# Attention scores in bursts of two duos over six PSUM banks, one routing scatter per step, in a fused attention and expert kernel

## The reference

```
x = x + tanh(g_xattn) * attention(layernorm(x), ctx, mask)   # 16 heads of 64
x = x + tanh(g_ffn)   * experts(layernorm(x))                # 8 experts, 2 per row

attention: q = ln(x) Wq, k = ctx Wk, v = ctx Wv
           softmax(q k^T / 8, masked) v Wo
experts:   top 2 of ln(x) Wg^T, softmax over the two,
           sum of weight * W3[e] (silu(W1[e] x) * (W2[e] x))
```

## Time and profile before

| what | value |
|---|---|
| median of three runs | 665.11 us (661.04 to 665.76) |
| the profiled execution | 661.78 us, span 660.0 us |
| busy share PE, DVE, ACT, POOL | 94%, 60%, 44%, 47% |
| chain that ended last, by engine | PE 77%, POOL 6%, DMA 5%, issue 4%, DVE 4% |
| attention steps 0 to 127 (from 33.0 to 402.6 us) | PE busy nearly without a gap |
| 402 to 432 us (end of attention) | PE busy 23.4 of 30.0 us, DMA share 0.99 |
| 480 to 640 us (expert tiles) | PE busy 160.0 of 160.0 us |

### The profile page before, as it was taken

The page is one execution under the profiler, slowest core; times in us unless marked ns, Lnnn a source line. Parts: engine busy times, 40 slices in busy tenths (PEclk is TensorE's granted clock), DMA queues, the critical chain, the costliest instruction groups (busy, mean ns, idle before and its releaser), DMA issues.

```text
span 660.0 us, 10752 instructions
## 1 busy us (share of the span) xinstructions
PE 622.1 (94%) x2958; PEld 346.2 (52%) x2959; DVE 393.6 (60%) x1187; ACT 287.7 (44%) x744; POOL 309.2 (47%) x272
## 2 busy tenths in 40 slices
PE   4599999999999999999999999699999999999994
PEld 2244445454555544455554555256666666666663
DVE  3767788888987878988769977333251212221211
ACT  1556665656555564564545554023322222222221
POOL 2345565555564587564685564502464222222221
PEclk9989999999999999999999998899999999999998
DMA  8904577676766776757677569969556322333221
GB/s 273 333 1 104 144 168 170 142 167 146 163 149 150 161 186 163 166 130 184 134 193 179 135 158 249 269 186 377 161 142 131 49 41 42 47 48 48 46 23 22
DMA packets 92652, 95.37 MB, mean 144 GB/s; under 512 B 11056, under 2 KB 86704, under 8 KB 92592
## 3 DMA queue, kind: packets, MB, share of 16 engines
q1 hardware_dynamic: 69968, 71.64, 41.9%
q10 hardware_dynamic: 15840, 14.07, 9.4%
q0 software_dynamic: 6784, 8.95, 8.2%
HBM read 27.72 MB, written 12.36 MB: 61 GB/s over the span
## 4 chain that ended last, share of the span: by engine, by line
PE 77%; POOL 6%; DMA 5%; issue 4%; DVE 4%; ACT 2%; ACTq 1%; POOLq 0%; SPq 0%; DVEq 0%
PE ps_s L1396 17%; PE ps_s L1216 14%; PE ps_o L1241 13%; PE ps_o L1424 8%; PE ps_a L1149 7%; PE ps_a L1251 7%; POOL probs L525 3%; POOL x_regrouped L513 2%; DMA out_dram<-yg,ids 2%; PE ps_o L1227 2%; PE ps_t L1417 2%; PE ps_s L1143 2%; DVE blocksT L996 2%; DMA probsT<-blocksT 1%; DMA wk_sb<-Wk_dram 1%
## 5 line engine op out<-in xcount | busy, mean ns | idle before, releaser
L525 POOL TENSOR_TENSOR probs<-probs,inv_sum 128x802 f32<-128x802 f32 x128 | 194.8, 1524 | 154.5 <-DVE inv_sum L975 153.7
L636 ACT ACTIVATE probs<-probs,neg_max 128x401 f32<-128x401 f32 x256 | 159.3, 624 | 147.1 <-DVE neg_max L984 147.0
L984 DVE CUSTOM_DVE_ANT_0 probs<-ps_s,biases 128x401 f32<-128x401 f32 x256 | 136.9, 573 | 52.5 <-PE ps_s L1216 51.6
L1396 PE MATMUL ps_s<-w_sb,xgT 128*128 x296 | 139.5, 594 | 1.4 <-ACT xgT L732 1.4
L996 DVE STREAM_TRANSPOSE blocksT<-probs 128x832 f32<-128x832 f32 x128 | 133.2, 1040 | 9.0 <-POOL probs L525 9.0
L564 POOL DMA_INDIRECT out_dram<-yg,ids x36 | 56.0, 1555 | 159.4 <-DVE yg L1108 136.5
L1241 PE MATMUL ps_o<-probsT,v_sb 128*64 128x512 f32 x512 | 125.0, 612 | 4.4 <-DMA probsT<-blocksT 4.4
L1216 PEld LDWEIGHTS ps_s<-kT,qT 64*128 64x128 f32 x1024 | 82.9, 187 | 78.6 <-DVE neg_max L984 42.2
L1216 PE MATMUL ps_s<-kT,qT 64*128 64x201 f32 (+1 forms) x1024 | 122.0, 357 | 1.4 <-issue 1.4
L1096 DVE TENSOR_TENSOR gated<-ps_s,silu 128x512 f32<-128x512 f32 x37 | 25.6, 692 | 117.5 <-PE ps_s L1396 112.1
L1396 PEld LDWEIGHTS ps_s<-w_sb,xgT 128*128 128x128 f32 x296 | 53.0, 191 | 39.5 <-issue 37.9
(11 more groups left out here) (142 smaller groups left out, 420.9 us busy)
## 6 DMA issues: line engine op xcount, KB each, us to landing
probsT<-blocksT SPq DMA_DIRECT2D x285, 96.0 KB
probsT<-blocksT SPq DMA_DIRECT2D x95, 128.0 KB
probsT<-blocksT ACTq DMA_DIRECT2D x99, 96.0 KB
xg<-x_regrouped SPq DMA_DIRECT2D x39, 129.0 KB, 2.1
probsT<-blocksT ACTq DMA_DIRECT2D x33, 128.0 KB
w_sb<-W1T_dram SPq DMA_DIRECT2D x8, 512.0 KB, 9.5
w_sb<-W2T_dram SPq DMA_DIRECT2D x8, 512.0 KB, 10.2
w_sb<-W3T_dram SPq DMA_DIRECT2D x8, 512.0 KB, 10.5
```

Of the source, the lines that this page charges most:

```text
L525: pool.tensor_tensor(duo, duo, inv_sum[:, u:u + 2].unsqueeze(2).to_broadcast([P, 2, LASTK]), ALU.mult)\
L636: act.activation(probs[:, b, 0:LASTK], probs[:, b, 0:LASTK], ACT.Exp, bias=neg_max[:, b:b + 1], scale=-1.0, accum_out=sum_exp[:, b:b + 1]) ...
L984: dve.tensor_tensor_reduce(probs[:, b, 0:LASTK], ps_s[u % 4][:, 0:LASTK], biases[:, tile, :], HD ** -0.5, 3e38, ALU.add, ALU.min, neg_max[ ...
L1396: mm = pe.matmul(bank[:, :], xgT[:, buf, k, :], w_sb[:, bass.ds(expert, 1), (n * KT + k) * FH:(n * KT + k + 1) * FH].squeeze(1), start=(k ...
```

## The change

There are six score banks, `ps_ring`, made of the four `ps_s` and the two `ps_t`. In an even step TensorE issues the scores of duos n and n + 1 one after the other, and in an odd step none. `scores(d)` now waits for the mask of duo d - 3. Everything else keeps its step. Since `ps_t` is taken, the late transposes of normalised x go to `ps_o` and `ps_a` by turns (`xn_bank`), with waits: in steps 8 to 10 for all value copies and for the queries' copy; the queries of step 9 for six of the eight transposes' copies; the queries of step 13 and the first `probs_v` for all eight.

In routing, row groups 0 and 1 (and 3, and the general path) scatter once per stage over stages 22 to 29, row group 2 still twice per stage over 22 to 25. `BESIDE` puts two such stages beside each of the expert tiles 6 to 9, so row group 3 keeps two scatters per tile.

```diff
-LAST_STAGE = 25
-BESIDE = (..., (22,), (23,), (24,), (25,))
+LAST_STAGE = 29
+BESIDE = (..., (22, 23), (24, 25), (26, 27), (28, 29))
...
+        ps_ring = ps_s + ps_t
+        def xn_bank(c):
+            return ps_t[c] if c < 2 else [ps_o, ps_a][c % 2]
...
-                if 22 <= s < 22 + GT:
-                    t = s - 22
-                    for c in range(2):
+                each = 2 if isinstance(r, int) and r == NR - 2 else 1
+                for n in range(each * (s - 22), each * (s - 21)):
+                    if 0 <= n < 2 * GT:
+                        t, c = divmod(n, 2)
                         pool.indirect_dma_start(...)
...
-                    if d >= 2:
-                        pe.wait_ge(masked_ready, 2 * d - 2)
+                    if d >= 3:
+                        pe.wait_ge(masked_ready, 2 * d - 4)
-                            mm = pe.matmul(ps_s[(2 * d + odd) % 4][:, k0:k1], ...
+                            mm = pe.matmul(ps_ring[(2 * d + odd) % 6][:, k0:k1], ...
...
                         if c == 0:
                             pe.wait_ge(v_ready, 2 * NS)
+                            pe.wait_ge(xnT_ready, 2 * NR)
...
-                    if n < DUOS:
+                    if n % 2 == 0 and n < DUOS:
                         scores(n)
+                        scores(n + 1)
                     if n < 2 * NS:
                         values(n)
                     if 2 * NS <= n < 2 * NS + 3:
+                        pe.wait_ge(v_ready, 2 * NS)
+                        pe.wait_ge(q_ready, (n + 2) // 4 + 1)
                         transpose_xn(2 * (n - 2 * NS) + 2)
                         transpose_xn(2 * (n - 2 * NS) + 3)
...
-                        if n // 4 + 1 == HP:
+                        if n == 2 * NS + 1:
+                            pe.wait_ge(xnT_ready, 6)
+                        if n // 4 + 1 == 4:
                             pe.wait_ge(xnT_ready, 2 * NR)
```

More of the change, by code:

```diff
@@ L61 @@
 ROUTE0 = HP * GT + 15
-LAST_STAGE = 25
-BESIDE = ((0, 1, 2, 3), (4, 5, 6, 7), (8, 9, 10), (12, 13, 14), (15, 16), (17, 18, 19, 20, 21), (22,), (23,), (24,), (25,))
+LAST_STAGE = 29
+BESIDE = ((0, 1, 2, 3), (4, 5, 6, 7), (8, 9, 10), (12, 13, 14), (15, 16), (17, 18, 19, 20, 21), (22, 23), (24, 25), (26, 27), (28, 29))
 SCHED_TILES = {7: range(0, 10), 8: range(10, 21)}
@@ L596, in move_xnT @@
                 act.wait_ge(xnT_ps, c + 1)
-                act.copy(xnT[:, c % 2, c // 2 * GQ:(c // 2 + 1) * GQ], ps_t[c % 2][:, :]).then_inc(xnT_ready, 1)
+                act.copy(xnT[:, c % 2, c // 2 * GQ:(c // 2 + 1) * GQ], xn_bank(c)[:, :]).then_inc(xnT_ready, 1)
             def mask_words(c):
@@ L983, in mask_and_max @@
                             dve.wait_ge(blocks_ready, (u - RING_P) // 2 + 1)
-                        dve.tensor_tensor_reduce(probs[:, b, 0:LASTK], ps_s[u % 4][:, 0:LASTK], biases[:, tile, :],
+                        dve.tensor_tensor_reduce(probs[:, b, 0:LASTK], ps_ring[u % 6][:, 0:LASTK], biases[:, tile, :],
                                                  HD ** -0.5, 3e38, ALU.add, ALU.min, neg_max[:, b:b + 1])\
@@ L1159, in transpose_xn @@
                     tile = xn[:, t, :] if c < 2 else xn_late[:, t0 - GT + t, :]
-                    mm = pe.transpose(ps_t[c % 2][:, t * P:(t + 1) * P], tile[:, k * P:(k + 1) * P], ident[:, :])
+                    mm = pe.transpose(xn_bank(c)[:, t * P:(t + 1) * P], tile[:, k * P:(k + 1) * P], ident[:, :])
                 mm.then_inc(xnT_ps, 1)
@@ L1215, in scores @@
                             h0 = odd * HD
-                            mm = pe.matmul(ps_s[(2 * d + odd) % 4][:, k0:k1], qT[h0:h0 + HD, c % 2, t * P:(t + 1) * P],
+                            mm = pe.matmul(ps_ring[(2 * d + odd) % 6][:, k0:k1], qT[h0:h0 + HD, c % 2, t * P:(t + 1) * P],
                                            kT[h0:h0 + HD, c % HP, k0:k1], start=True, stop=True)
```

## The result

The changed kernel takes 658.48 us (median of 8 runs, 656.09 to 660.88) against 665.01 us of the kernel before (8 runs, 661.04 to 666.78): a ratio of 0.9907 with a 95% interval of 0.9881 to 0.9934, 6.2 us less. The profiled execution took 659.66 us, with a span of 657.9.

A forecast was written before the change was run, and what follows sets the result against it. PE, busy 93.00 of 93.00 us in plain attention steps, was taken as the bound, DVE next at 84%. Terms summed to -4.8 us, 661.8 to 657.0, put at 658.6 between run levels; forecast's own range 653 to 663, overall 650 to 668.

The forecast's parts named there:

- Seams: Steady periods: 6 seams for 8 at about 0.2 us each, 11.1 to 10.7 us, -10.8 over 27; list ends -0.4.
- Scatters: Row groups 0 and 1: with one scatter per stage both output-projection stalls, 1.38 and 1.62 us, go: -3.0 us.
- Slack of the queries' copy: New period: ACT's queries copy has 0.9 us to spare; routing stages lose 0.3 us per row group, +0.8 in all.
- the walk: The prediction's engine-by-engine timing from a burst's start, for one new period and for steps 8 to 11.
- Rival C: Queries' copy misses its slack in every period, 0.6 us net each in 27 periods: about 675 us; chance 0.08.
- B: DVE or ACT becomes the bound in routing stages, half of 10.8 us lost, sum +0.6: about 663 us; chance 0.17.
- Steps 0 to 7 and 8 to 11: Early steps: four value pairs wait for ACT's copy on one bank, +1.4 us; transposes without own banks, +3.7 us.
- Routing groups: Waits for ACT's copies: stage 9 transposes +0.85 in row groups 0 to 2, +2.6; stage 17 counts +0.9 us.
- The sum: All terms over the whole kernel: -4.8 us, from the profiled 661.8 to 657.0, then 658.6 as median.
- the two levels of the runs: Runs before: median 3.3 us above the profiled execution, one run at 661.0 like it; new median put half-way.
- Rival A: Half of the 8.6 us of new waits, or 4 us from cheaper seams, sum -9: about 654 us; chance 0.2.
- D: Bursts pulled apart by the second duo's wait for a mask: about 668 us; chance 0.03.

The follow-up runs named there:

- e5: On the kernel of e3, output projection and queries together behind one burst, both probs_v halves behind the next; 655.55 us, ratio 0.9877 to the kernel before.
- e2: The kernel before with only one scatter per stage for row groups 0 and 1, no bursts; 661.62 us, ratio 0.9956.
- e1: The changed kernel with two scatters per stage again for row groups 0 and 1; 664.72 us, ratio 1.0019 to the kernel before.
- e3: The changed kernel with steps 0 to 11 in their old order and banks, bursts from step 12 only; 653.75 us, ratio 0.9837 to the kernel before.

## Why the prediction was right, point by point

**Seams, -10.8 and -0.4.** Right. 10.70 for 10.7 us a period, and the free choice of 0.18 for the unseen seam between output projection and probs_v holds: 1.93 to the next start. e5 confirms the count.

**Scatters, -3.0.** Right for what it was priced as, the two waits of before: e2 gives -3.0. It was incomplete as a description of the change: in bursts the same two scatters would cost 8.0 (e1), so the scatter edit is what makes the bursts pay at all. I had worked out POOL's pace against PE's for the new number of scatters only.

**Slack of the queries' copy.** Right, though thinner than the walk had it: in the period shown above the copy ends at 93.25, 6.3 us behind the burst at 86.96 for 6.0, and leaves 0.6 us for 0.9. Only one wait of 0.26 us showed, for an assumed 0.8 over three row groups. Rival C is refuted by 10.69 us in nearly every plain period, and B, an engine other than PE as the bound of the routing stages, by the middle period of each row group, which fell from 12.97 to 12.55 us. e1 shows what C would have looked like. Two prices among the rivals were added up wrongly. C's 0.6 us of net cost replaces the gain of 10.8 and does not stand beside it, so its time would be some 11 us above the 675 given. B's sum of +0.6, put between the levels as the forecast was, is 664 and not 663.

**Steps 0 to 7 and 8 to 11, +1.4 and +3.7.** 5.1 forecast. The first probs_v comes 5.5 us later in the two first profiles, and e3 returns 5.1 of the whole way to the counts. The waits are those of the walk: 0.73 per value pair for 0.75, then 0.90, 1.47 and 1.91 for ACT's copies. The split is less exact. Steps 0 to 7 lost 2.0 us for 1.4: two value groups with a wait between them return nothing by merging (2.71 us from the start of one, 45.08, to the next, 47.79, for 1.91 before), so that a pair lost 0.6 and not 0.36, while the last pair lost nothing, because its wait was there before. Steps 8 to 11 lost 3.5 for 3.7.

**Routing groups, +2.6 and +0.9.** The waits are 3 x 0.77 and 2 x 0.37, 3.1 for 3.5. From queries to queries these periods lost more than their brackets: beside a plain period 1.15, 1.0 and 1.0 us with the transposes of stage 9 and twice 0.44 with the counts, 4.0 in all. The 0.26 of the slack is in it, so 4.0 stands for 2.6 + 0.9 + 0.8 = 4.3.

**The sum.** To the counts behind step 128 it was -4.8 forecast and 374.3 - 369.8 = -4.5 measured, or 374.7 - 369.8 = -4.9 over the mean of two and three profiles. The whole kernel gained 6.2 us by the ratio, from 1.3 to 1.7 more than that. The interval of the ratio reaches from 4.4 to 7.9 us, so the surplus may be nothing but scatter. If it is real, its source stays open: the part behind the attention steps took 252.6 to 254.6 us in the five profiles of these two kernels, with no clear difference between them, and a longer form of it (31.5 us from counts to tile) was seen once, in e2. The forecast of 658.6 stood 6.5 us under the median before, of which the sum gave 4.8 and my choice to put the median between the two levels of the runs 1.7. That choice was a guess, and that the median of 658.48 came out so near to it is luck.

**Rival A** (waits cheaper than the walk, seams free) did not come about; **D** neither.

## What to carry to other kernels

Count the places where TensorE changes between row tiles, column tiles and the full array, and price each from a place in the trace where two like groups already touch; here it is 0.2 us each, and grouping like matmuls returned 0.4 us of an 11 us period twice. Where matmuls are moved together, find for each engine in strict order what each copy stands behind: wherever a cover was taken away (from the value copies, the shared banks, the rowsT copy), the wait showed at nearly its full length. When one edit quickens an engine and another relieves its neighbour, measure them apart: either half alone gave -3.0 or +3.5 us, both -4.5.

## What the runs showed of the hardware

A wait of 2.2 to 2.5 us of TensorE in e1 was followed by a stretch of 3.6 us at a mean granted clock of 0.67, so that such a wait cost about 4 us in all. The first expert tile fell on either level. In the changed kernel's first profile its first eight matmul records took 5.39 us, at a clock of 0.68, and in the two others 3.69, at 1.00. This alone makes the 1.7 us between executions in the last column of the table.

It goes with the idle time just ahead of the tile's first transposes, behind the last output projection. Where PE stood still there for 1.25 to 1.47 us (the first profile of the changed kernel, e1, e3), the records took 5.39 us, and where it did for 4.47 (e5), 6.62. Where it did for 0.96 us or less, in the ten other profiles, the records took 3.69 to 3.70. The long form of the end in e2 is of the same kind: the last two chunks' probs_v wait 3.56 and 3.62 us for their transfers, for 2.13 and 2.24 in the kernel before, and the second time the sixteen matmuls behind the wait take 6.61 us for 3.65.
